# The neighbour aggregate ahead of router and ranks on TensorE, in a graph network with a routed expert layer

## What is computed

```python
# block 1, for each graph
n   = layernorm(x)
agg = eps * n + adj @ n                       # the aggregate
h   = silu(rmsnorm(agg @ W1 + b1) * rms_w)    # 128 -> 512
x   = x + h @ W2 + b2                         # 512 -> 128
# block 2, for each token
f      = layernorm(x)
logits = f @ router_w.T                       # 8 experts, the best 2 are taken
x      = x + sum over the 2 of gate * expert_mlp(f)
```

## Time and profile before

| | us |
|---|---|
| median of three runs | 579.77 |
| the runs | 579.54 to 584.45 |
| time of the profiled execution | 586.93 |
| span of that execution, first to last instruction | 584.9 |
| PE busy | 503.6 (86%) |
| DVE busy | 396.8 (68%) |
| ACT busy | 316.6 (54%) |
| POOL busy | 342.1 (58%) |
| granted TensorE clock, mean | 0.942 |

### The profile page before, as it was taken

The page is one execution under the profiler, slowest core; times in us unless marked ns, Lnnn a source line. Parts: engine busy times, 40 slices in busy tenths (PEclk is TensorE's granted clock), DMA queues, the critical chain, the costliest instruction groups (busy, mean ns, idle before and its releaser), DMA issues.

```text
span 584.9 us, 13139 instructions
## 1 busy us (share of the span) xinstructions
PE 503.6 (86%) x3841; PEld 468.2 (80%) x3859; DVE 396.8 (68%) x1482; ACT 316.6 (54%) x701; POOL 342.1 (58%) x337
## 2 busy tenths in 40 slices
PE   4899887788878877987485899999999999999990
PEld 3688776677766766877485799999999999999990
DVE  4477767667757766776354676677777777777764
ACT  2477566555655665653234355555555555555551
POOL 4225675756657675766445466666666666666662
PEclk9799899988989999897797899999999999999995
DMA  6232434242232425112612222334344444443534
GB/s 178 73 114 74 135 92 125 70 133 81 82 111 90 129 81 182 36 38 55 166 45 93 74 67 76 101 110 128 121 133 122 123 128 127 119 127 118 166 93 126
DMA packets 39319, 62.01 MB, mean 106 GB/s; under 512 B 8295, under 2 KB 24938, under 8 KB 39158
## 3 DMA queue, kind: packets, MB, share of 16 engines
q1 hardware_dynamic: 29926, 43.23, 25.9%
q0 software_dynamic: 8640, 17.84, 9.0%
q10 hardware_dynamic: 720, 0.53, 0.3%
HBM read 36.49 MB, written 26.15 MB: 107 GB/s over the span
## 4 chain that ended last, share of the span: by engine, by line
PE 75%; ACT 7%; issue 5%; DVE 4%; another core or an unknown queue 4%; DMA 3%; POOL 1%; ACTq 0%; POOLq 0%; SPq 0%; DVEq 0%
PE routing_ps L954 16%; PE y_ps L816 9%; PE up_ps L937 9%; PE up_ps L935 9%; PE up_ps L936 8%; PE up_ps L799 4%; PE up_ps L785 3%; PE up_ps L797 3%; PE y_ps L922 3%; PE routing_ps L775 3%; ACT squares L651 2%; PE up_ps L798 2%; PE up_ps L796 2%; ACT hidden_t L635 1%
## 5 line engine op out<-in xcount | busy, mean ns | idle before, releaser
L607 POOL DMA_INDIRECT results<-result,slot_rows x142 | 162.0, 1141 | 103.6 <-DVE result L1394 80.7
L935 PE MATMUL up_ps<-rows_lo,up_hi 128*114 128x256 f32 x426 | 127.5, 299 | 10.0 <-issue 8.0
L937 PE MATMUL up_ps<-rows_hi,up_hi 128*114 128x256 f32 x426 | 121.5, 285 | 0.0
L936 PE MATMUL up_ps<-rows_hi,up_lo 128*114 128x256 f32 x426 | 121.4, 285 | 0.0
L724 ACT ACTIVATE scaled<-up_ps 114x768 f32<-114x768 f32 x71 | 57.6, 811 | 107.0 <-issue 77.9
L954 PE MATMUL routing_ps<-ew_sb,hidden_t 114*128 x852 | 107.9, 277 | 1.7 <-DVE result L1394 1.7
L954 PEld LDWEIGHTS routing_ps<-ew_sb,hidden_t 114*128 114x128 f32 x852 | 101.5, 193 | 2.4 <-issue 2.4
L559 POOL TENSOR_TENSOR inverse<-spreads,minus_half 128x6 f32<-128x6 f32 (+2 forms) x37 | 46.3, 1250 | 80.0 <-DVE spreads L1010 74.4
L935 PEld LDWEIGHTS up_ps<-rows_lo,up_hi 128*114 128x114 f32 x426 | 77.3, 181 | 11.1 <-issue 8.7
L1379 DVE TENSOR_TENSOR rows_lo<-y_ps,rows_hi 128x256 fp32r<-128x256 f32 x71 | 30.1, 424 | 80.5 <-ACT rows_hi L729 69.1
L567 POOL DMA_INDIRECT expert_rows<-rows,slot x64 | 65.2, 1019 | 28.8 <-issue 17.2
(11 more groups left out here) (182 smaller groups left out, 881.1 us busy)
## 6 DMA issues: line engine op xcount, KB each, us to landing
slot_rows<-expert_rows SPq DMA_DIRECT2D x71, 130.0 KB
adj<-in_adj_t SPq DMA_DIRECT2D x32, 256.0 KB
adj<-results SPq DMA_DIRECT2D x14, 512.0 KB
tokens<-in_x SPq DMA_DIRECT2D x32, 128.0 KB
out<-tokens SPq DMA_DIRECT2D x16, 256.0 KB
ew_sb<-in_ew SPq DMA_DIRECT2D x6, 456.0 KB
results<-result,slot_rows POOLq DMA_INDIRECT x142
expert_rows<-rows,slot POOLq DMA_INDIRECT x128
```

The lines of the kernel that those rows point to most:

```text
L607: pool.indirect_dma_start(out=results[0:SPARE + (GROUPS - first_group(i)) * GROUP_ROWS, :], out_offset=bass.IndirectOffsetOnAxis(ap=slot_r ...
L935: pe.matmul(part, up_hi[:, r, at], rows_lo[:, r, :], start=True, stop=False)
L936: pe.matmul(part, up_lo[:, r, at], rows_hi[:, r, :], start=False, stop=False)
L937: ins = pe.matmul(part, up_hi[:, r, at], rows_hi[:, r, :], start=False, stop=True)
```

## The change

In PE's `step`, the call of `sum_neighbours(j+2)` moves from the last place to the place behind the two `transpose_hidden`, ahead of `router(j-2)` and `rank(j-3)`. No instruction is added or removed, no wait is changed, and no other engine's list differs.

```diff
--- before.py
+++ after.py
@@ -857,14 +857,14 @@
                 if j.within(GRAPHS):
                     transpose_hidden(j, 0)
                     transpose_hidden(j, 1)
+                if j.plus(2).within(GRAPHS):
+                    sum_neighbours(j.plus(2))
                 if j.plus(-2).within(GRAPHS):
                     router(j.plus(-2))
                 if is_last(j, SPLIT + 3) and j.off == SPLIT + 3:
                     count_rows(early_count_ps, SPLIT_GROUPS)
                 if j.plus(-3).within(GRAPHS):
                     rank(j.plus(-3))
-                if j.plus(2).within(GRAPHS):
-                    sum_neighbours(j.plus(2))
 
             def count_rows(ps, groups):
```

## The result

| | before | with the change |
|---|---|---|
| median, us (4 runs each, same chip) | 581.3 | 604.07 |
| runs, us | 579.54 to 584.45 | 603.68 to 606.37 |
| ratio, 95% interval | 1 | 1.0394 (1.0335 to 1.0452) |
| span of the profiled execution, us | 584.9 | 602.0 |
| PE busy, us | 503.6 | 515.2 |

The change makes the kernel 22.8 us slower. The forecast was 582 with a range up to 590, so it was wrong. The side was that of rival 1, whose middle was 590, the size about twice what that rival gave.

A forecast was written before the change was run, and what follows sets the result against it. PE was taken to bound the graph stage from 34 to 60 us, then a ring through POOL. With (a), (c) and (e) at 0, (b) paid in steps 2 to 4 and 29 gave +2 us: 579.8 to 582, range 575 to 590.

The forecast's parts named there:

- rival 1: Late ranks delay DVE's place, carried round the ring into the next step's squares: 587 to 592, middle 590; chance 0.23.
- What bounds the kernel: Graph stage: PE is the bound from 34 to 60 us; from 60 to 242 us a ring through POOL sets the pace.
- both regimes: Graph stage: PE busy 25.52 of 26 us from 34 to 60 us, then 153.51 of 182 us to 242 us.
- the ring: Graph stage from 60 us: scatters, squares, mean square, inverse, scatters again; inverse starts 6.61 to 9.41 us apart.
- (a): PE's aggregate starts 0.47 us earlier in a step, but releases nothing that ends a wait: worth 0.
- (b): PE's router and ranks start 0.95 us later; the second product then waits for the logits copy: 0.45 us idle.
- (d): Where PE's idle time is paid: steps 2 to 4, 1.35 us, and step 29, about 0.5; sum about 2 us.
- (c): DVE's place, shift and low half come 0.95 us later in step 4; PE does not feel it, by 0.15 us.
- (e): Steps 5 to 28: later place and second product taken as 0, covered by the late arrival of PE's results.
- Rival 2: PE's results arrive when its records say; all 28 steps from 2 to 29 pay 0.45: 12.6 us, 592; chance 0.04.
- Rival 3: Later second product changes whether squares pass before results are held; five to seven steps become short, middle 574; chance 0.13.
- Rival 4: ACT's and DVE's aggregate halves take data sooner and the first product waits for them, giving back (b): 580; chance 0.1.

The follow-up runs named there:

- e5: Kernel before without POOL's four scatters a step, two small memsets raising their semaphores instead: 523.61 us, 0.903 of the kernel before.
- e12: Kernel before with the two scatters of the second choices dropped and those of the first choices kept: 528.25 us, 0.900 of the kernel before.

## Why the prediction was wrong

- **What bounds the kernel**: right, both regimes. e5 and e12 show what was only read before: in the second regime the ring runs through the scatters.
- **(a)** right. In step 4 ACT's high half starts right behind the silus, 0.07 us after their end (52.22 against 52.15) where it was 0.62 before (51.92 against 51.30), and nobody could use it; the shift stands in front of the low half.
- **(b)** right in kind, a little small in size: 0.57 us a step without scatters and 0.46 on the other kind of chip, for 0.45. The sum let PE follow the logits copy at once; it follows after 0.25 us. The written-out steps 2 to 4 became 7.05, 6.93 and 6.94 us long against 6.17, 6.52 and 6.38 (starts of the first scaling pass), 1.85 us for the 1.35 of the sum (d). For step 29 the sum had 0.5; steps 29 and 30 together lost 0.1, step 28 1.3.
- **(c)** right: in step 4 the low half ends at 54.75, and PE takes up the first product, which needs it, at 55.17 with no idle time ahead.
- **(e)** is the step that failed: "I take 0 for these, with the cover named: the late arrival of PE's results." The late arrival is no cover. A square that has not got in ahead of the last scatter is held until 0.9 to 1.1 us behind its end in most steps. Before the change both squares got in in 6 of the loop's steps (6.6 to 7.8 us) and the first in 9 (8.3 to 8.7). With PE and DVE later by 0.5 to 0.9 us both squares, with the copy of the rows between them, are held in 16 steps (9.1 to 9.6 us). What I held to be slack was a door that closes. The loop, which the sum had at 0, lost 18.5 us, 0.92 a step on average. And where nothing is late the term isn't 0 either: without scatters each step pays 0.57 us.
- **Rival 1** had the side right, and that lateness is carried round the ring, and was priced by 11 steps of 0.5 to 0.95. The number of steps was taken from a wait of the profile before; with the change the pattern itself moved, and 18 of the loop's 20 steps are longer than they were, from scaling pass to scaling pass. Its sign, squares released by PE directly, didn't come: they are released behind the scatters. Its middle was 590, the result 604.
- **Rival 2**, no hiding at all at 592, is what happens where the results are not late: 1.0251. The case against it, "182 us in which PE is idle for 28", was a wrong inference. Idle time of PE in a step says that PE isn't the bound, not that PE's lateness is free. The rule of the Trainium skill by which it was named (SBUF — State Buffer, the section on SBUF's two sides) agrees with the second kind of chip, where the squares follow PE with a scatter running. The first kind does not agree: steps of 6.5 us instead of 8.2 to 8.3 when half of the scatters go. Whether it is at SBUF that the results are delayed, no run shows.
- **Rival 3** named the mechanism that the runs show: what sets a step's length is whether the squares pass before the results are held, and a later second product changes which it is. It had the side wrong. It expected short steps to be gained, and the change took all 6 away: the shortest loop step is 8.3 us now. It said itself that the pattern could go either way, and priced only the one. **Rival 4** fell with (a).

## What to carry to other kernels

An engine's last work in a step can be what covers a round trip. Before moving it, ask what then stands directly behind what: here the ranks' matmuls came to stand in front of a product that waits for another engine to read them, and the price was that round trip, some 0.5 us, in every step in which PE is the bound. And where an engine idles in a ring that other engines set, lateness on it is not free: take the fastest and the slowest step of the pattern, find what tells them apart, and price the change as all steps becoming the slowest. Here that would have been 20 x (9.4 - 8.3) = 22 us, from the longest period and the mean step of the profile before; the loop lost 18.5.

## What the runs showed of the hardware

The same kernel took 524 us on two chips and 580 to 587 on three others. On the slower kind, while POOL's scatters ran, ACT's squares started up to 3.5 us behind the start of the PE matmul that they wait for, against 0.4 to 0.5 where nothing was late. They mostly came 0.9 to 1.1 us behind the end of the last scatter, some of the first squares right behind the third; with two of the four scatters removed the median was 0.8. On the faster kind, with the same scatters, it was 0.5 to 0.7. What in a scatter delays PE's results, and why on some chips only, is open. The time between DVE's logits copy and PE's next matmul that waits for it was 0.25 us. No version tried here beats the kernel before on either kind.
